# A transformer block on one core: the last two key tiles of each softmax denominator added by an accumulating DMA

## The reference

```python
tp = silu(time_emb) @ Wt + bt            # shift, scale, gate, twice
h = layernorm(x, g1, be1) * (1.0 + scale_msa) + shift_msa
q, k, v = split(h @ Wqkv + bqkv)         # 16 heads of 32
attn = softmax(einsum('blhd,bmhd->bhlm', q, k) * scale, axis=-1)
h = einsum('bhlm,bmhd->blhd', attn, v) @ Wproj + bproj
x = x + gate_msa * h
h = layernorm(x, g2, be2) * (1.0 + scale_mlp) + shift_mlp
x = x + gate_mlp * (gelu(h @ W1 + b1) @ W2 + b2)
```

## Time and profile before

| | |
|---|---|
| median of 3 runs | 4009.19 us (4009.13 to 4010.85) |
| the profiled execution | 4011.15 us |
| its span, first to last instruction | 4009.4 us |
| mean granted clock of TensorE | 0.993 |
| instructions | 51892 |

### The profile page before, as it was taken

The page is one execution under the profiler, slowest core; times in us unless marked ns, Lnnn a source line. Parts: engine busy times, 40 slices in busy tenths (PEclk is TensorE's granted clock), DMA queues, the critical chain, the costliest instruction groups (busy, mean ns, idle before and its releaser), DMA issues.

```text
span 4009.4 us, 51892 instructions
## 1 busy us (share of the span) xinstructions
PE 3947.7 (98%) x19723; PEld 2717.3 (68%) x19723; DVE 2414.3 (60%) x4020; ACT 1812.7 (45%) x3220; POOL 1927.4 (48%) x562
## 2 busy tenths in 40 slices
PE   8999999999999999999999999999999999999998
PEld 6777886445555555555555554788888888888886
DVE  3665557787878878787887875333443433344442
ACT  2222223666666666666666666333333333333332
POOL 1000004788888888887888888632112222221221
PEclk9999999999999999999999999999999999999999
DMA  5444463333233233323323332411011112111110
GB/s 197 180 180 163 185 218 94 75 70 77 59 88 75 65 76 78 79 59 88 75 65 77 78 80 64 124 35 43 35 43 35 48 40 66 43 35 43 35 43 21
DMA packets 184996, 323.72 MB, mean 81 GB/s; under 512 B 14452, under 2 KB 53428, under 8 KB 184748
## 3 DMA queue, kind: packets, MB, share of 16 engines
q1 hardware_dynamic: 184748, 320.41, 28.0%
HBM read 201.77 MB, written 117.54 MB: 80 GB/s over the span
## 4 chain that ended last, share of the span: by engine, by line
PE 93%; DVE 3%; DMA 2%; issue 1%; ACT 1%; POOL 0%; SPq 0%; POOLq 0%; ACTq 0%; DVEq 0%
PE psum L997 12%; PE psum L535 12%; PE psum L1008 12%; PE psum L436 10%; PE psum L437 10%; PE psum L438 10%; PE psum L1519 6%; PE psum L1515 6%; PE psum L1517 6%; PE psum L1024 5%; PE psum L1038 4%; DVE max_part L825 2%; PE psum L1477 1%; PE psum L471 1%; PE psum L543 0%
## 5 line engine op out<-in xcount | busy, mean ns | idle before, releaser
L825 DVE TENSOR_REDUCE max_part<-psum 128x1 f32<-128x512 f32 x2048 | 1288.6, 682 | 299.2 <-PE psum L535 292.7
L1118 ACT ACTIVATE probs<-psum 128x512 f32<-128x512 f32 x2048 | 1095.0, 599 | 619.3 <-PE psum L997 609.5
L1226 POOL TENSOR_TENSOR prob_sum<-prob_sum,probs 128x2048 f32<-128x2048 f32 x256 | 1176.8, 4597 | 29.5 <-ACT probs L1118 0.9
L535 PE MATMUL psum<-k_stack,q_stack 96*128 96x512 f32 x2048 | 771.5, 407 | 3.7 <-DVE max_part L825 1.7
L1648 DVE TENSOR_TENSOR g_parts<-g_full,g_parts 128x512 fp32r<-128x512 f32 x256 | 263.2, 1028 | 818.3 <-ACT g_parts L1557 818.3
L997 PE MATMUL psum<-q_stack,k_stack 98*128 98x512 f32 x2048 | 741.2, 408 | 4.9 <-issue 3.8
L997 PEld LDWEIGHTS psum<-q_stack,k_stack 98*128 98x128 f32 x2048 | 383.2, 190 | 247.6 <-issue 109.8
L1553 ACT ACTIVATE g_full<-psum,cols 128x512 f32<-128x512 f32 x256 | 176.6, 690 | 815.7 <-PE psum L438 815.4
L1715 POOL TENSOR_TENSOR y_out<-y_out,rows 128x512 f32<-128x512 f32 x64 | 82.9, 1296 | 936.4 <-DVE y_out L1686 936.4
L535 PEld LDWEIGHTS psum<-k_stack,q_stack 96*128 96x128 f32 x2048 | 383.3, 190 | 208.4 <-DVE max_part L825 122.8
L1008 PE MATMUL psum<-probs,v_group 128*32 128x512 f32 x4096 | 503.6, 598 | 0.0
(11 more groups left out here) (152 smaller groups left out, 4759.9 us busy)
## 6 DMA issues: line engine op xcount, KB each, us to landing
qk_parts<-qk_out SPq DMA_DIRECT2D x128, 512.0 KB, 2.8
k_stack<-qk_parts SPq DMA_DIRECT2D x96, 512.0 KB, 7.1
q_stack<-qk_parts SPq DMA_DIRECT2D x192, 256.0 KB, 9.4
x_in<-in_x SPq DMA_DIRECT2D x16, 1024.0 KB, 5.4
v_rows<-v_out SPq DMA_DIRECT2D x64, 256.0 KB, 2.0
v_group<-v_rows SPq DMA_DIRECT2D x32, 512.0 KB, 4.0
gated_attention<-gated SPq DMA_DIRECT2D x64, 256.0 KB, 4.6
x<-in_x SPq DMA_DIRECT2D x16, 1024.0 KB, 8.2
```

What stands on the lines that cost most here:

```text
L535: pe.matmul(psum[:, SMAX[at.turn % 3], :], q_stack[u % 3][0:PARTS, h, i * P:(i + 1) * P], k_stack[G % 2][0:PARTS, h, kh * CH:(kh + 1) * CH ...
L825: dve.reduce_max(max_part[:, n:n + 1], psum[:, SMAX[at.turn % 3], :], AX.X).then_inc(dve_smax, 1)
L1118: act.activation(probs[slot(u, kt)][:, h, :], psum[:, ST[n % 3], :], ACT.Exp, scale=SCALE).then_inc(act_exp, 1)
L1226: pool.tensor_tensor(total[:, :, :], total[:, :, :], probs[slot(u, kt)][:, :, :], ALU.add).then_inc(pool_sum, 1)
```

## The change

Each unit makes two denominator groups instead of three. POOL sums tiles 0 to 5 in place, into the buffer of tile 0. Then, early in the next unit, when all exps and all V of the unit are done, it issues a DMA that adds the buffer of tile 6 to that of tile 7 (128 x 2048 float32, 1 MB, `accum_op=ALU.add`, both in SBUF). D1 is the summed tile 0, D2 the merged tile 7, which waits for that DMA. The two `prob_sum` buffers and the ring of six become eight buffers: one of its own for each of tiles 2, 3, 5, 6 and 7, and three that go round among tiles 0, 1 and 4, so that a sum in tile 0 lives on while the next unit begins. ACT's wait for a free buffer is rewritten for it. Wproj's raw load, formerly in `prob_sum[0]`, goes to `probs_round[0]`, and ACT waits for its split before the first exp. ORDER is another string; with it LEAD falls from 16 to 10. In the last unit the merge is issued after the first projection part of `pool_tail`, and D2 stands after the second projected tile.

```diff
-    ORDER = ("sgmsmsmsmDsmsmmssmasVDmssmsmmswDVtmrmmspssmVVV!n"
-             "VssmjmjmjjsjmsmssmjmjsmsjmjssmsmjsjmsmmjsssmmVV")
+    ORDER = ("smsmsmgsmwVVsmmmasssmVsmsmsmsmsDssmsmsmsmsmVmsm"
+             "ssmmsmsVtDrpnVVV!mssjmjmjsmjmjssmsjmjsmsjmjjmjj")
-    AHEAD = 0
-    LEAD = N_MAX + AHEAD - ORDER.split("!")[0].count("m")
+    LEAD = N_MAX - ORDER.split("!")[0].count("m")
-    RING = 6
+    ROUND_TILES = (0, 1, 4)
+    BEFORE = {0: 1, 1: 4, 4: 0}
...
+        def probs(u, kt):
+            if kt in ROUND_TILES:
+                return probs_round[(u + ROUND_TILES.index(kt) + 1) % 3]
+            return probs_own[kt]
...
         def pe_denominators(pe, u, n):
-            term = prob_sum[u % 2] if n == 2 else probs[slot(u, SUMMED + n)]
             if n == 0:
...
-            if n == 2:
                 pe.wait_ge(pool_sum, sums_done(u, SUMMED - 1))
+                term = probs(u, 0)
+            else:
+                pe.wait_ge(a_merge[u % 2], 16 * (u // 2 + 1))
+                term = probs(u, LAST)
...
+        def act_wait_for_buffer(act, u, kt):
+            act.wait_ge(pe_pv, u * KT + kt + 1)
+            if kt == 0:
+                act.wait_ge(pe_den, 2 * u + 1)
+            elif kt < SUMMED:
+                act.wait_ge(pool_sum, sums_done(u, kt))
+            elif kt == SUMMED:
+                act.wait_ge(a_merge[u % 2], 16 * (u // 2 + 1))
+            else:
+                act.wait_ge(pe_den, 2 * u + 2)
...
-                        if h == 0 and k >= RING:
...
+                        if h == 0 and u:
+                            act_wait_for_buffer(act, u - 1, BEFORE.get(kt, kt))
...
+        def pool_merge(pool, u):
+            pool.wait_ge(act_exp, KT * (u + 1) * GH)
+            pool.wait_ge(pe_pv, KT * (u + 1))
+            pool.dma_start(out=probs(u, LAST)[:, :, :], in_=probs(u, SUMMED)[:, :, :],
+                           accum_op=ALU.add).then_inc(a_merge[u % 2], 16)
...
             for u in range(NU):
-                total = prob_sum[u % 2]
+                if u:
+                    pool_merge(pool, u - 1)
+                total = probs(u, 0)
                 for kt in range(1, SUMMED):
                     pool.wait_ge(act_exp, (u * KT + kt + 1) * GH)
                     if kt == 1:
-                        if u >= 2:
-                            pool.wait_ge(pe_den, 3 * (u - 1))
-                        pool.tensor_tensor(total[:, :, :], probs[slot(u, 0)][:, :, :],
-                                           probs[slot(u, 1)][:, :, :],
-                                           ALU.add).then_inc(pool_sum, 1)
+                        pool.wait_ge(pe_pv, u * KT + 1)
...
             pe_denominators(pe, NU - 1, 0)
+            pe_project(pe, at + 1, tail_bank(at + 1))
             pe_denominators(pe, NU - 1, 1)
-            pe_project(pe, at + 1, tail_bank(at + 1))
-            pe_denominators(pe, NU - 1, 2)
...
             pool_project(pool, TAIL[0])
+            pool_merge(pool, NU - 1)
```

More of the change, by code:

```diff
@@ L162, in build_block @@
         negmax_lo = early("negmax_lo", [GH * TT, P], fp32r)
-        prob_sum = [early("prob_sum0", [P, GH, CH])]
+        probs_round = [early("probs_round0", [P, GH, CH])]
         wproj_hi = wproj_region("wproj_hi", [P, KD, D], fp32r)
@@ L172, in build_block @@
         v_group.append(s2("v_group1", [P, KT, P]))
-        prob_sum.append(s2("prob_sum1", [P, GH, CH]))
-        probs = [s2(f"probs{i}", [P, GH, CH]) for i in range(RING)]
+        probs_round += [s2(f"probs_round{i}", [P, GH, CH]) for i in (1, 2)]
+        probs_own = {kt: s2(f"probs{kt}", [P, GH, CH]) for kt in range(KT)
+                     if kt not in ROUND_TILES}
         attn = [s2("attn_other", [P, NG, L]), project_region("attn_last", [P, NG, L])]
@@ L257, in build_block @@
         a_gated, a_g = sems("a_gated", 2), sems("a_g", 2)
+        a_merge = sems("a_merge", 2)
         a_wr, act_w12, pool_w12 = sems("a_wr", 3), sem("act_w12"), sem("pool_w12")
@@ L384, in sp_early_load @@
             elif j == 4:
-                sp.dma_start(prob_sum[0][:, :, :],
+                sp.dma_start(probs_round[0][:, :, :],
                              t["Wproj"].rearrange("(k p) n -> p k n", p=P)).then_inc(a_wproj, 16)
@@ L425, in ring_of_send @@
                 return N_MAX
-            return min(N_MAX * (u + 1) + AHEAD, N_MAX * NU) + u
+            return N_MAX * (u + 1) + u
         def three_pass(pe, dst, terms, between=None):
@@ L609, in act_stage1 @@
                     act.wait_ge(side_free, 16)
-                    act.activation(wproj_hi[:, :, :], prob_sum[0][:, :, :],
+                    act.activation(wproj_hi[:, :, :], probs_round[0][:, :, :],
                                    ACT.Copy).then_inc(act_wprojhi, 1)
@@ L872, in dve_stage1 @@
                     dve.wait_ge(act_wprojhi, 1)
-                    dve.tensor_tensor(wproj_lo[:, :, :], prob_sum[0][:, :, :],
+                    dve.tensor_tensor(wproj_lo[:, :, :], probs_round[0][:, :, :],
                                       wproj_hi[:, :, :].bitcast(fp32),
@@ L1009, in pe_values @@
                               v_group[G % 2][:, kt, h * HD:(h + 1) * HD],
-                              probs[slot(u, kt)][:, h, :], start=kt == 0, stop=kt == LAST)
+                              probs(u, kt)[:, h, :], start=kt == 0, stop=kt == LAST)
             i.then_inc(pe_pv, 1)
         def pe_denominators(pe, u, n):
-            term = prob_sum[u % 2] if n == 2 else probs[slot(u, SUMMED + n)]
             if n == 0:
@@ L1020, in pe_denominators @@
                     pe.wait_ge(dve_attn, u)
-            if n == 2:
                 pe.wait_ge(pool_sum, sums_done(u, SUMMED - 1))
+                term = probs(u, 0)
+            else:
+                pe.wait_ge(a_merge[u % 2], 16 * (u // 2 + 1))
+                term = probs(u, LAST)
             for h in range(GH):
                 i = pe.matmul(psum[h * HD:(h + 1) * HD, DEN_BANK, :], ones[:, :], term[:, h, :],
-                              start=n == 0, stop=n == 2)
+                              start=n == 0, stop=n == 1)
             i.then_inc(pe_den, 1)
@@ L1098, in act_attention @@
             act.wait_ge(dve_evict1, NC * 12)
+            act.wait_ge(dve_wprojlo, 1)
             for i in range(3):
@@ L1130, in dve_turn @@
         def dve_turn(dve, u):
-            dve.wait_ge(pe_den, 3 * (u + 1))
+            dve.wait_ge(pe_den, 2 * (u + 1))
             if u:
@@ L1312, in sp_tail @@
             store_gated(sp, TAIL[0])
-            sp.wait_ge(pe_den, 3 * NU)
+            sp.wait_ge(pe_den, 2 * NU)
             sp.wait_ge(pool_sum, sums_done(NU - 1, SUMMED - 1))
@@ L1348, in act_tail @@
                 act_project(act, TAIL[n])
-            act.wait_ge(pe_den, 3 * NU)
+            act.wait_ge(pe_den, 2 * NU)
             act.wait_ge(pool_sum, sums_done(NU - 1, SUMMED - 1))
@@ L1375, in dve_tail @@
             dve_normalise_attention(dve, NU - 1)
-            dve.wait_ge(pe_den, 3 * NU)
+            dve.wait_ge(pe_den, 2 * NU)
             dve.wait_ge(pool_sum, sums_done(NU - 1, SUMMED - 1))
@@ L1409, in pool_tail @@
                 pool_residual_part(pool, 0, n - 1)
-            pool.wait_ge(pe_den, 3 * NU)
+            pool.wait_ge(pe_den, 2 * NU)
             pool.wait_ge(act_weighted, NU)
```

18 lines of the change are left out of this document (4 added, 14 removed).

## The result

The changed kernel takes 3945.26 us (median of 4 runs, 3945.03 to 3949.16) against 4010.02 us before (4 runs, 4009.13 to 4011.03): a ratio of 0.9838, 95% interval 0.9826 to 0.9849. That is 64.8 us less. The forecast was 3954 us with a range from 3947, so the sign and most of the mechanism held and the size did not.

A forecast was written before the change was run, and what follows sets the result against it. PE (TensorE), busy 98% of the span, was taken as the bound. From the median of 4009.2 us, minus 56 for the removed group, plus 1 for the ends: 3954 us, range 3947 to 3965.

The forecast's parts named there:

- Part 1: PE in the attention units: one denominator group less saves 0.90 us in each of 62 units, 56 us.
- The changes cost the same in both: PE's order: five runs of fp32 groups before and five after, so changes of kind add no difference.
- The price of the group: PE: one fp32 group inside a run, taken from pieces of three and two groups, costs 0.90 to 0.93 us.
- Rival D: The group is not worth its 0.90 us because PE then waits for exps or maxima; 4001 to 4009 us, chance 0.06.
- +1 for the ends: Last unit and tail: late POOL, the last merge and moved maxima together cost 1 us.
- Part 2: POOL: issuing the merge holds it 1.3 us (bounds 0.4 and 4.6), hidden in its idle time; in-place sums cost nothing new.
- Part 3: Merge landing before D2: 7.6 us alone, ready at 12.7 in odd units, 16.5 in even ones; D2 starts at 17.4.
- The other end of the forecast: Merge transfer in a cheap-second-read case: 1 MB lands in 5.2 us instead of 7.6.
- rival A: Even units: merge shares engines evenly with the keys, D2 is 2.9 us late, 90 us lost, 4044 us; chance 0.12.
- the two thirds of the forecast: Even units: the merge's longer rows give it two thirds of the DMA engines, landing at 16.5 us.
- The reasoning about the values: Even units: values, issued at 3.8 instead of 11.2, count among 8.9 us of other transfers due at the merge's start.
- Rivals B and C: B: small D2 delay or long POOL hold, 3980 us, chance 0.14; C: slow accumulating transfer, 4124 us, chance 0.08.

The follow-up runs named there:

- b_turn: Kernel before with the turn of the maxima behind the fourth V of its run instead of the third, n ahead of it: 3990.36 us, 0.9947.
- a_turn: Changed kernel with the turn one V earlier, between the second and third V of its run: 3965.44 us, 0.9885.
- b_less_block: Kernel before without the second denominator group, which stands in a run behind a V (tile 7 left out): 3958.08 us, 0.9866.
- a_alone: Changed kernel without its merge transfer (tile 6 left out of the denominators): 3943.93 us, 0.9829.
- b_both: Kernel before without the second denominator group (tile 7 left out) and with the turn at the end of its run: 3934.09 us, 0.9810.
- a_pair: Changed kernel with the first D moved up behind the third V, making one run of two groups: 3949.00 us, 0.9847.
- a_vlate: Changed kernel with only the letter of the values' load moved; it was still issued at the same time: 3947.46 us, 0.9843.
- a_copy: Changed kernel with a plain copy of the same size and queue in place of the accumulating transfer: 3944.55 us, 0.9834.
- a_vlate2: Changed kernel with the values' load of even units made to wait for a later V, so issued after the merge: 3943.92 us, 0.9836.
- a_early: Changed kernel with its second D and the turn t behind it 11 letters earlier, 13.8 us into the unit instead of 17.4: 4117.01 us, 1.0263.

## Why the prediction missed, point by point

**Part 1 was mis-sized, and this is the miss.** The step that failed is "The changes cost the same in both". It counted the runs (five and five, right) and took the turn for a part of a run without a price of its own, so the term stood at nothing. The turn costs 0.34 us between two V and next to nothing at the end of a run; the new order moved it there: 62 x 0.34 = 21 us, shown in both directions by b_turn and a_turn. The trace of the kernel before had it, in the rows of 1207 to 1211 us shown above, which the forecast didn't use. The price of the group was off too, by less: the piece of 24 has 2.71 us beside that of 16 with 1.85, so the third group is 0.86, and dividing by three or two mixed the end of the run into the price of a group. At 0.86 (b_less_block) the group is worth 53 us and not 56.

These two make 74 us. That the forecast is off by 9 us and not by 18 is luck: the next term, which it did not have either, has the other sign.

**What took 9 us of that back.** 0.86 + 0.34 = 1.20 us a unit, of which 1.11 arrived. The missing 0.09 are shown by a_alone and b_both to be the new order's and not the merge's. Some of its alternating s and m follow each other at 0.24 to 0.27 us instead of 0.233 (after the lone D, 1213 to 1215 us in the changed kernel, and again in a_pair), and from 1100 to 1567 us the weight loads of scores wait 37.5 us for exps in a_alone where they wait 13.4 in b_both. Part of these waits is hidden behind PE's work; that they are all of the 0.09 was not shown. Rival D had named this wait, with a far higher price. At the ends: the first exp comes at 649.8 us instead of 652.2 (1.1 of these 2.4 us are there before any maximum, at the last transposes of the first stage, and are no part of the change); from there to the tail's first projection matmul the stage took 65.1 us less (2509.62 - 652.16 against 2442.11 - 649.77), where 62 x 1.105 are 68.5, so the first and the last two units lost 3.4; behind that matmul 1.8 us more (4009.4 - 2509.62 against 3943.7 - 2442.11). Sum: -2.4 - 65.1 + 1.8 = -65.7 us, the difference of the spans. The forecast had +1 for the ends. These small terms are less certain than they look: the first exp came at 652.0 us in a_alone and at 651.8 in a_vlate, which have the changed kernel's order string, and the 1.8 us were not followed up.

**Part 2 was right.** POOL is held for 0.88 us (forecast 1.3, bounds 0.4 and 4.6), the first sum's place is not disturbed, and 2.6 us of idle remain in a unit (2.4 forecast). In-place sums take 4.6 us as before.

**Part 3 was right, with less cover than it said.** The merge lands after 7.3 us in the odd unit (7.6 forecast); what the addition costs is shown by a_copy. The other end of the forecast was misadded: 2.0 us for 256 KB and 0.8 for each further 256 KB make 4.4 us for 1 MB and not 5.2, and the copy took 4.6. The Trainium skill ("Collectives: The Full Stack", on reduce-scatter) has an adding transfer at half the rate of a copy. With the fixed 1.2 us of the forecast taken off both, which is an estimate from the earlier trace rows, the merge is (7.3 - 1.2) / (4.6 - 1.2) = 1.8 times as long as the copy here, so this case's trace comes near it. In even units it has 12.4 us, 1.7 times the time alone: by that estimate the merge gets some six tenths of the engines, between the half of rival A and the two thirds of the forecast. It is issued 4.45 us into the unit and not 5.1, takes 12.4 us and not 11.4, and so lands after 16.9, against 16.5 forecast and D2 at 17.4; two errors partly cancel. (The 8.9 us of other transfers come out as 11.7 - 5.1 + 2 = 8.6; nothing hangs on it.) The reasoning about the values was wrong in one point: they do not compete with the merge (a_vlate2).

**Rival A was near.** Had the engines been shared evenly, D2 would have been late; a_early shows that the price would have been higher than the 90 us I gave it, since I named the clock but added nothing for it. Rivals B and C did not happen; a PE that waited 1.4 us in all for the merge excludes both.

**The range** named 0.93 us a group for its lower end, but that gives 4009.2 - 62 x 0.93 = 3951.5 us and not 3947. By its own working the range was missed by 6 us and not by 1.7. It did not contain the chance that the new order string itself was better than the old one. A rewritten order is a part of the change with a price of its own, on either side.

## What to carry to other kernels

When an order of instructions is rewritten, price every kind of neighbour pair on the bound engine from start to start, the rare instructions too: here one small transposition of 128 x 16 cost 0.34 us or 0.03 by its place, and one of them in each unit made a third of the gain. The pauses that a costly instruction gives to other engines can be worth something: the lone group was 1.18 us on PE and 0.70 in the end. An accumulating DMA can take an addition from the bound engine for nothing, if its landing is covered at the worst traffic of the cycle and not at the mean: here 7.3 us alone, 12.4 beside a large load.

## What was not expected of the hardware

- A transposition by PE between two groups of fp32 matmuls cost 0.34 us, at the end of such a run 0.03 (rows above), though it is 0.28 us long in both places.
- A transfer of 1 MB from SBUF to SBUF with addition takes 7.3 us, the copy 4.6 in the same place (odd unit, 1228 to 1256 us), and POOL is held for 0.87 us against 0.57.
- In a_early PE kept a granted clock of 1.00 after 2.72 us of idle, had 0.60 over the next 4.3 us after 3.19, and 0.50 over the next 8.3 us after 3.35. Nearly the same idle time cost 3.1 us in one unit and 8.2 in another.
